# Other slots between the scans for a state-space layer's neighbouring work, and exponentials four slots ahead

## The chip, the cores and the metric

The kernel is one launch on one core of a Trainium2 chip. The metric is the device time of that launch in microseconds. TensorE (PE) multiplies and transposes, VectorE (DVE) and ScalarE (ACT) do elementwise work, GpSimd (POOL) too, and SyncE (SP) starts transfers. Each engine runs its own instructions in their order and waits on semaphores for the others.

## The reference

A decoder layer in float32: a state-space block, a cross-attention and a mixture of experts, each behind a layer norm and with a residual. The change lies in the state-space block alone:

```
xz = einsum('bld,ed->ble', layernorm(x), in_proj_w);  xp, z = xz[..., :ED], xz[..., ED:]
xc = silu(causal depthwise conv of xp over 4 positions)
dt, Bm, Cm = split(einsum('ble,fe->blf', xc, x_proj_w))
delta = softplus(dt @ dt_proj_w.T + dt_proj_b);  A = -exp(A_log)
dA = exp(delta[..., None] * A);  BX = delta[..., None] * Bm[:, :, None, :] * xc[..., None]
hs[t] = dA[t] * hs[t-1] + BX[t]
y = einsum('blen,bln->ble', hs, Cm) + D * xc
x = x + einsum('ble,de->bld', y * silu(z), out_proj_w)
```

x is 4 x 1024 x 256, ED is 512, there are N = 16 states and R = 64 ranks of dt.

## The kernel before, in words

`mamba_phase` cuts the 4 x 1024 positions into NCH = 8 chunks of 512 positions (CT), two to a sequence. Channels lie on partitions: ED = 512 gives KE = 4 blocks. A chunk has STEPS = 64 scans, one for each state n and block e; scan k is one VectorE instruction over 512 positions (`scan`, L485). Every scan is the centre of one **slot**. Each engine's program is written by the same double loop, `slots`: chunk h, slot s, and for each slot the function `slot` of that engine, which puts the slot's own instructions first and then whatever of other work has that slot's number.

For scan k the engines do this. ScalarE computes the decay, `a_step` (L369, exp of delta times A), into `a_ring`, six tiles deep, AHEAD slots ahead of the scan, and the input in turned form, `scale_u` (L381), into `bxT`, KE slots further ahead. TensorE turns bxT into one of two PSUM banks one slot ahead (`bx`, L576). VectorE scans. GpSimd multiplies two scans' results by C in one instruction, `pair` (L324), into `hc_ring`. TensorE turns and sums these products in PSUM, `y` (L593), LAG = 5 slots behind. The exponential of scan k waits until scan k-6 has left the ring; the turn for scan k until scan k-2 has left its bank.

Between these stands the work of the neighbours, by a table of slot numbers. While chunk h is scanned, chunk h+1 is prepared: XT turns the normalised input (TensorE, copied by ScalarE), IN projects it (two matmuls in two slots for each of four blocks), CONV is VectorE's convolution in four steps from the slot named, Z projects the gate (two slots for each of four tiles; VectorE copies it two slots later, L542), at SILU_AT ScalarE does a silu of xc (L433) and of zT (L437) with a table load before and after, XP projects xc to dt, B and C (four slots; ScalarE copies it to `xd_rows` four slots later, L361), BT turns those rows, DT projects dt (VectorE takes the minimum one slot later, L548, ScalarE the exponential and logarithm of the softplus, L386 and L390, VectorE the maximum four slots later, L552), U is GpSimd's delta times xc (L350), UT turns it and ScalarE copies it to `uT` (L361). Of chunk h-1, GATE multiplies y by silu(z) (L530), YT turns it, OUT projects it (four slots for each half, L684; VectorE adds the residual four slots after its number, L560). Of chunk h+2, LN takes the norm's statistics, AGGR aggregates them (L520), EPS adds the epsilon (L523, L524), RSTD is ScalarE's root (L400, L402), APPLY is GpSimd's four normalising instructions (L332). D adds D * xc (L602).

IN, Z, XP, DT, UT, YT, OUT, XT and BT share two PSUM banks (`bank_of`). The tuple `order` gives the order in which they fill them; every fill waits until the one before in its bank is emptied (`wait_emptied`).

The attention and the experts follow; the first parts of the attention stand in the last slots (`ATTEND_AT`).

## Time and profile before

| | |
|---|---|
| runs | 2038.38 us median of 3 (2036.39 to 2042.06) |
| profiled execution | 2040.1 us, its span 2038.0 us |
| PE busy | 1864.1 us, 91% of the span |
| DVE busy | 1166.3 us, 57% |
| ACT busy | 1101.7 us, 54% |
| POOL busy | 1100.7 us, 54% |
| mean granted TensorE clock | 0.978 |

Matmul busy time counts pipelined instructions by modelled ends, so a busy PE is not PE at its peak. The shares are over the whole span; the state-space part is the first 43% of it. A timeline row gives the start, the time taken, the engine and the line, what is written from what, and in brackets how long the engine had been idle and who ended that. Consecutive instructions of one kind are one row with their count. Durations of instructions that follow each other without a gap overlap by some 0.1 us, so the distance of two starts is the better measure. A "chunk" below is a value of h, its slots are counted from 0.

### The profile page before, as it was taken

The numbers are of one execution on the slowest core, as the hardware profiler recorded it, in microseconds if no ns is written. First come the engines' busy times: TensorE is split into PE (matmuls) and PEld (weight loads), VectorE is DVE, ScalarE is ACT, GpSimd is POOL, SyncE is SP. The second block draws the span as 40 slices with busy tenths as digits, with TensorE's granted clock in tenths as the row PEclk, the third lists the DMA queues.
The fourth block names the chain that finished last, engine by engine and source line by source line (L and its number), as shares of the span: only waits on it lengthen the run. The fifth ranks groups of instructions, "written<-read, shape, count | busy, mean of one in ns | idle before, by whom it ended". The sixth has DMA issues, their size and how long they took to land. (4 is left out here: it accounts for less than half of the span.)

```text
span 2038.0 us, 29493 instructions
## 1 busy us (share of the span) xinstructions
PE 1864.1 (91%) x10630; PEld 1518.1 (74%) x10630; DVE 1166.3 (57%) x1760; ACT 1101.7 (54%) x2157; POOL 1100.7 (54%) x806
## 2 busy tenths in 40 slices
PE   5888998989998998878999993999999999999998
PEld 2666676767676767766666652888888888888897
DVE  4899998999999998975677763111111111111111
ACT  3898989898989989944767761111111111111111
POOL 1686878778787878845667874222222222222131
PEclk8999999999999999999999995999999999999999
DMA  4121211112121113101111012974344444434451
GB/s 118 36 64 42 64 52 64 53 42 73 43 73 43 63 43 96 48 22 47 32 32 53 22 43 59 358 244 145 107 137 120 113 145 109 142 114 112 137 153 16
DMA packets 100019, 177.21 MB, mean 87 GB/s; under 512 B 24307, under 2 KB 70771, under 8 KB 89876
## 3 DMA queue, kind: packets, MB, share of 16 engines
q1 hardware_dynamic: 84196, 156.63, 22.9%
q0 software_dynamic: 15680, 18.69, 5.5%
q8 instruction: 87, 1.43, 0.3%
q14 instruction: 56, 0.46, 0.1%
HBM read 152.81 MB, written 22.82 MB: 86 GB/s over the span
## 5 line engine op out<-in xcount | busy, mean ns | idle before, releaser
L324 POOL TENSOR_TENSOR m_hc_ring<-m_h_ring,m_c_bc 128x1024 f32<-128x1024 f32 x256 | 606.3, 2374 | 127.8 <-DVE m_h_ring L485 109.6
L1825 PE MATMUL e_ps<-e_xT,e_w 128*128 128x256 f32 (+1 forms) x2560 | 501.0, 356 | 0.8 <-ACT e_xT L1753 0.8
L1825 PEld LDWEIGHTS e_ps<-e_xT,e_w 128*128 128x128 f32 x2560 | 440.9, 191 | 51.3 <-issue 1.2
L1737 POOL DMA_INDIRECT out<-e_y,e_who x71 | 113.4, 1597 | 552.3 <-DVE e_y L1789 449.5
L576 PEld LDWEIGHTS m_ps<-m_ident,m_bxT 128*128 128x128 f32 x2048 | 234.8, 141 | 216.6 <-DVE m_h_ring L485 102.6
L369 ACT ACTIVATE m_a_ring<-m_delta,m_negA 128x512 f32<-128x512 f32 x512 | 366.1, 716 | 39.5 <-DVE m_h_ring L485 39.1
L576 PE MATMUL m_ps<-m_ident,m_bxT 128*128 128x128 f32 x2048 | 320.6, 279 | 67.8 <-DVE m_h_ring L485 61.7
L381 ACT ACTIVATE m_bxT<-m_uT,m_bT 128x512 f32<-128x512 f32 x512 | 364.5, 712 | 0.0
L1780 DVE TENSOR_TENSOR e_hT<-e_gact,e_ps 128x512 f32<-128x512 f32 x142 | 97.7, 688 | 453.5 <-ACT e_gact L1762 453.5
L485 DVE TENSOR_TENSOR_SCAN m_h_ring<-m_a_ring,m_carry,m_ps 128x512 f32<-128x512 f32 x256 | 316.8, 1267 | 27.4 <-ACT m_a_ring L369 13.3
L485 DVE TENSOR_TENSOR_SCAN m_h_ring<-m_a_ring,m_ps 128x512 f32<-128x512 f32 x256 | 304.1, 1209 | 35.7 <-PE m_ps L576 14.1
L593 PE MATMUL m_ps<-m_ident,m_hc_ring 128*128 128x128 f32 x2048 | 309.5, 276 | 0.8
L1762 ACT ACTIVATE e_gact<-e_ps 128x512 f32<-128x512 f32 x142 | 84.8, 597 | 414.5 <-PE e_ps L1825 414.5
L1838 PE MATMUL e_ps<-e_w,e_hT 128*128 x1136 | 251.8, 379 | 1.6 <-issue 1.6
L593 PEld LDWEIGHTS m_ps<-m_ident,m_hc_ring 128*128 128x128 f32 x2048 | 242.9, 142 | 2.5 <-DVE m_zT L530 2.4
L1838 PEld LDWEIGHTS e_ps<-e_w,e_hT 128*128 128x128 f32 x1136 | 215.1, 190 | 30.6 <-issue 1.7
L1753 ACT ACTIVATE e_xT<-e_ps 128x512 f32<-128x512 f32 (+1 forms) x40 | 22.0, 549 | 260.0 <-PE e_ps L1812 260.0
L1789 DVE TENSOR_SCALAR e_y<-e_ps,e_meta 128x256 f32<-128x256 f32 x71 | 31.5, 480 | 194.4 <-PE e_ps L1838 194.4
L1031 ACT ACTIVATE t_probs<-m_ps,t_nmax 128x77 f32<-128x77 f32 x512 | 118.6, 369 | 10.1 <-DVE t_nmax L1208 10.1
L937 POOL TENSOR_TENSOR t_probs<-t_probs,t_rtotal 128x616 f32<-128x616 f32 x64 | 77.8, 1217 | 82.9 <-DVE t_rtotal L1202 80.5
L1505 PE MATMUL m_ps<-t_k_blk,t_qT 128*128 128x308 f32 x256 | 78.8, 430 | 7.0 <-ACT t_qT L1120 4.1
L1728 POOL DMA_INDIRECT e_xg<-xn,e_who x71 | 71.1, 1001 | 20.7 <-POOL e_who L1725 11.0
(195 smaller groups left out, 2077.4 us busy)
## 6 DMA issues: line engine op xcount, KB each, us to landing
e_w<-in_gate_up_w SPq DMA_DIRECT2D x78, 1024.0 KB, 6.8
m_c_bc<-c_rows SPq DMA_DIRECT2D x32, 1024.0 KB, 6.0
e_w<-in_down_w SPq DMA_DIRECT2D x8, 1024.0 KB
m_x_in<-in_x SPq DMA_DIRECT2D x8, 512.0 KB, 5.7
m_x_res<-in_x SPq DMA_DIRECT2D x8, 512.0 KB, 6.7
x<-m_x_res SPq DMA_DIRECT2D x8, 512.0 KB, 2.9
t_xa<-x SPq DMA_DIRECT2D x8, 512.0 KB
out<-t_xa SPq DMA_DIRECT2D x8, 512.0 KB
```

Of the source, the lines that this page charges most:

```text
L324: p.tensor_tensor(hc_ring[:, k % HC, :, :], h_ring[:, n % 2, e:e + 2, :], c_bc[:, n, :].unsqueeze(1).to_broadcast([P, 2, CT]), ALU.mult).t ...
L369: a.activation(a_ring[:, k % A_RING, :], delta[c % 2][:, e, :], ACT.Exp, scale=negA[:, e, n:n + 1]).then_inc(a_ready, 1)
L381: a.activation(bxT[:, row % BXT, i, :], uT[c % 2][:, i, :], ACT.Copy, scale=bT[:, c % 2, i, n:n + 1]).then_inc(bxT_ready, 1)
L485: v.tensor_tensor_scan(h_ring[:, n % 2, e, :], a_ring[:, k % A_RING, :], ps[:, BX + k % 2, :], initial, ALU.mult, ALU.add).then_inc(scan_d ...
L576: last = t.transpose(out[:, i * P:(i + 1) * P], src(i), ident[:])
L593: last = t.matmul(ps[:, Y + i, e * P:(e + 1) * P], hc_ring[:, k // 2 % HC, e % 2, i * P:(i + 1) * P], ident[:], is_transpose=True, start=( ...
L1031: last = a.activation(dst[:, h, :], src[:, h // (HP // 2), h % (HP // 2), :], ACT.Exp, bias=nmax[:, g % 2, h:h + 1])
L1737: nc.gpsimd.indirect_dma_start(out=out, out_offset=bass.IndirectOffsetOnAxis(ap=who[:, tile:tile + 1], axis=0), in_=y[:, s % 2, i, :], in_ ...
L1762: nc.scalar.activation(gact[:, k % 2, :], gu_bank(s, g, 0), ACT.Gelu).then_inc(g_ready, 1)
L1780: nc.vector.tensor_tensor(h_out(s, g), gact[:, k % 2, :].rearrange("p (f t) -> p f t", f=n), gu_bank(s, g, 1).rearrange("p (f t) -> p f t" ...
L1825: last = t.matmul(gu_bank(s, g, which)[:, f * wide:(f + 1) * wide], w1[s % W1_RING][:, c, lo:lo + P], xT[:, s % 2, c, 0:wide], start=(c == ...
L1838: last = t.matmul(ps[:, Y_BANK + s % 2, i * D:(i + 1) * D], hT[:, s % 2, f, i * P:(i + 1) * P], w2[:, bass.ds(e, 1), f, :].rearrange("p a ...
```

## The change

The number of instructions stays; the table of slots and one constant change. The exponential (and with it bxT) is placed four slots ahead of its scan instead of three. CONV of the first block moves from slot 9 to 8, the second Z tile from 27 to 26, XP from 30 to 27, BT from 35 to 32, DT, U and UT three slots earlier (the last two UT: 49 and 51 become 46 and 48), the first half of OUT from 51 to 50. AGGR and EPS move from 56 and 57 to 60, RSTD from 59 to 62, APPLY from 60 to 63. `order` is now computed from the same table by sorting, with the result in the order of the slots.

```
--- before.py
+++ after.py
@@ -110,7 +110,7 @@
     TOTAL = NCH * STEPS
     ONE_ROW, C0, B0 = R, R + 32, R + 32 + N
     A_RING, BXT, HC = 6, 3, 4
-    AHEAD, LAG = 3, 5
+    AHEAD, LAG = 4, 5
     TAIL = KC - 1
     G = 4
     NG = N // G
@@ -182,9 +182,24 @@
 
         bank_of = {"XT": (0, 1), "IN": (0, 1, 0, 1), "YT": (0, 0, 0, 0), "Z": (1, 0, 1, 0), "XP": (1,), "BT": (0,),
                    "DT": (1, 0, 1, 0), "UT": (1, 0, 1, 0), "OUT": (1, 0)}
-        order = (("XT", 0), ("XT", 1), ("IN", 0), ("IN", 1), ("IN", 2), ("IN", 3), ("YT", 0), ("YT", 1), ("YT", 2),
-                 ("YT", 3), ("Z", 0), ("Z", 1), ("XP", 0), ("BT", 0), ("DT", 0), ("DT", 1), ("DT", 2), ("DT", 3),
-                 ("UT", 0), ("UT", 1), ("UT", 2), ("UT", 3), ("OUT", 0), ("OUT", 1), ("Z", 2), ("Z", 3))
+        LN_AT, AGGR_AT, EPS_AT, RSTD_AT, APPLY_AT = (51, 52, 53, 54), 60, 60, 62, 63
+        XT_AT = (1, 2)
+        GATE_AT = (5, 6)
+        IN_AT, CONV_AT = (5, 9, 13, 17), (8, 13, 17, 21)
+        D_AT = (7, 11, 15, 19)
+        YT_AT = (21, 22, 23, 24)
+        SILU_AT = 25
+        Z_AT = (25, 26, 59, 61)
+        XP_AT, BT_AT = 27, 32
+        DT_AT = (33, 34, 38, 39)
+        U_AT = (38, 39, 43, 45)
+        UT_AT = (43, 44, 46, 48)
+        OUT_AT = (50, 55)
+
+        fill_at = {"XT": XT_AT, "IN": IN_AT, "YT": YT_AT, "Z": Z_AT, "XP": (XP_AT,), "BT": (BT_AT,), "DT": DT_AT,
+                   "UT": UT_AT, "OUT": OUT_AT}
+        order = sorted(((kind, i) for kind, at in fill_at.items() for i in range(len(at))),
+                       key=lambda f: fill_at[f[0]][f[1]])
         nth, fills = {}, [0, 0]
         for h in range(-1, NCH + 1):
             for kind, i in order:
@@ -210,20 +225,6 @@
                         attend(g)
             for g in range(0, parts.last):
                 attend(g)
-
-        LN_AT, AGGR_AT, EPS_AT, RSTD_AT, APPLY_AT = (51, 52, 53, 54), 56, 57, 59, 60
-        XT_AT = (1, 2)
-        GATE_AT = (5, 6)
-        IN_AT, CONV_AT = (5, 9, 13, 17), (9, 13, 17, 21)
-        D_AT = (7, 11, 15, 19)
-        YT_AT = (21, 22, 23, 24)
-        SILU_AT = 25
-        Z_AT = (25, 27, 59, 61)
-        XP_AT, BT_AT = 30, 35
-        DT_AT = (36, 37, 41, 42)
-        U_AT = (41, 42, 46, 48)
-        UT_AT = (46, 47, 49, 51)
-        OUT_AT = (51, 55)
 
         block = ctx.enter_context(nc.Block())
```

On TensorE, from the second half of the first Z tile to the first XP matmul. L654 is the z projection, L663 the x projection (line numbers of the changed kernel are one higher), L576 the turn of bxT, L593 that of the products; one turn and one product stand in each slot. Before:

```order
L654 MATMUL m_ps<-m_w_in,m_xnT 128x512
L576 MATMUL m_ps<-m_ident,m_bxT 128x128 x4
L593 MATMUL m_ps<-m_ident,m_hc_ring 128x128 x4
L654 MATMUL m_ps<-m_w_in,m_xnT 128x512
L576 MATMUL m_ps<-m_ident,m_bxT 128x128 x4
L593 MATMUL m_ps<-m_ident,m_hc_ring 128x128 x4
L654 MATMUL m_ps<-m_w_in,m_xnT 128x512
L576 MATMUL m_ps<-m_ident,m_bxT 128x128 x4
L593 MATMUL m_ps<-m_ident,m_hc_ring 128x128 x4
L576 MATMUL m_ps<-m_ident,m_bxT 128x128 x4
L593 MATMUL m_ps<-m_ident,m_hc_ring 128x128 x4
L663 MATMUL m_ps<-m_xc,m_w_x 128x512
```

And now, from the first half of the first Z tile:

```order
L655 MATMUL m_ps<-m_w_in,m_xnT 128x512
L577 MATMUL m_ps<-m_ident,m_bxT 128x128 x4
L594 MATMUL m_ps<-m_ident,m_hc_ring 128x128 x4
L655 MATMUL m_ps<-m_w_in,m_xnT 128x512 x2
L577 MATMUL m_ps<-m_ident,m_bxT 128x128 x4
L594 MATMUL m_ps<-m_ident,m_hc_ring 128x128 x4
L655 MATMUL m_ps<-m_w_in,m_xnT 128x512
L664 MATMUL m_ps<-m_xc,m_w_x 128x512
L577 MATMUL m_ps<-m_ident,m_bxT 128x128 x4
L594 MATMUL m_ps<-m_ident,m_hc_ring 128x128 x4
L664 MATMUL m_ps<-m_xc,m_w_x 128x512
```

Four z matmuls in four slots, a free slot and then the x projection have become z matmuls in three slots with two of them in the second, and the x projection begins in the third.

On ScalarE, at the start of the first chunk's scans, behind the copies of uT. L369 is the exponential (a_ring), L381 is bxT, L400 and L402 are the norm's root. Before:

```order
L361 ACTIVATE m_uT_82<-m_ps 128x4x128 x4
L381 ACTIVATE m_bxT<-m_uT_82,m_bT 128x512 x3
L400 ACTIVATE m_rstd<-m_rstd 128x4
L402 ACTIVATE m_rstd<-m_rstd 128x4
L381 ACTIVATE m_bxT<-m_uT_82,m_bT 128x512
L369 ACTIVATE m_a_ring<-m_delta_80,m_negA 128x512
L381 ACTIVATE m_bxT<-m_uT_82,m_bT 128x512
L369 ACTIVATE m_a_ring<-m_delta_80,m_negA 128x512
```

And now:

```order
L362 ACTIVATE m_uT_82<-m_ps 128x4x128 x4
L382 ACTIVATE m_bxT<-m_uT_82,m_bT 128x512 x4
L370 ACTIVATE m_a_ring<-m_delta_80,m_negA 128x512
L382 ACTIVATE m_bxT<-m_uT_82,m_bT 128x512
L370 ACTIVATE m_a_ring<-m_delta_80,m_negA 128x512
L382 ACTIVATE m_bxT<-m_uT_82,m_bT 128x512
L370 ACTIVATE m_a_ring<-m_delta_80,m_negA 128x512
L382 ACTIVATE m_bxT<-m_uT_82,m_bT 128x512
L401 ACTIVATE m_rstd<-m_rstd 128x4
L403 ACTIVATE m_rstd<-m_rstd 128x4
L370 ACTIVATE m_a_ring<-m_delta_80,m_negA 128x512
```

The root stood behind three bxT; it now stands behind seven bxT and three exponentials.

## Rows read from the trace of the kernel before

**Rows 1.** Busy time by stretch (us, PE, PEld, DVE, ACT, POOL, PEclk, DMA share, GB/s)
```profile
56.40:885.90 829.50, 754.84 (x5176) 597.22 (x5173) 761.96 (x819) 756.21 (x1202) 660.48 (x396) 0.99 0.18 54
163.60:206.10 42.50, 38.40 (x280) 30.63 (x279) 42.50 (x50) 33.51 (x55) 30.26 (x13) 1.00 0.18 50
206.10:249.50 43.40, 38.98 (x259) 28.80 (x257) 39.65 (x40) 43.36 (x68) 35.40 (x18) 1.00 0.22 66
249.50:270.30 20.80, 20.80 (x136) 17.47 (x137) 18.05 (x25) 19.74 (x34) 17.03 (x12) 1.00 0.13 45
```

**Rows 2.** Timeline of ScalarE, chunk 1 (start us, us, engine, line, operation, count)
```profile
205.94 1.28 ACT L433 ACT_TABLE_LOAD   x1
...
212.27 0.72 ACT L369 ACTIVATE m_a_ring<-m_delta,m_negA 128x512 f32<-128x512 f32 x1
...
222.09 0.71 ACT L369 ACTIVATE m_a_ring<-m_delta,m_negA 128x512 f32<-128x512 f32 x1
```

**Rows 3.** Timeline of VectorE, chunk 1 (in brackets: idle before, and its releaser)
```profile
213.02 1.28 DVE L485 TENSOR_TENSOR_SCAN m_h_ring<-m_a_ring,m_carry,m_ps 128x512 f32<-128x512 f32 x1 [1.55 <-ACT m_a_ring L369]
...
261.53 1.28 DVE L485 TENSOR_TENSOR_SCAN m_h_ring<-m_a_ring,m_carry,m_ps 128x512 f32<-128x512 f32 x1 [0.46 <-PE m_ps L576]
```

**Rows 4.** Timeline of TensorE, chunk 1 and the start of chunk 2
```profile
205.59 0.66 PE L576 MATMUL m_ps<-m_ident,m_bxT 128*128 128x128 f32 x4 [0.30 <-DVE m_h_ring L485]
...
206.52 1.02 PE L654 MATMUL m_ps<-m_w_in,m_xnT 128*128 128x512 f32 x2
...
224.04 0.66 PE L576 MATMUL m_ps<-m_ident,m_xd_rows 128*128 128x128 f32 x4 [0.68 <-ACT m_xd_rows L361]
...
249.47 1.10 PE L684 MATMUL m_ps<-m_w_out,m_ygT 128*128 128x256 f32 x4 [0.61 <-ACT m_uT L361]
...
259.10 0.60 PE L576 MATMUL m_ps<-m_ident,m_bxT 128*128 128x128 f32 x4
...
260.84 0.60 PE L576 MATMUL m_ps<-m_ident,m_bxT 128*128 128x128 f32 x4
...
272.52 0.60 PE L576 MATMUL m_ps<-m_ident,m_x_in 128*128 128x128 f32 x4
```

**Rows 5.** Timeline of ScalarE, chunk 1: copies of xd_rows and of uT
```profile
223.32 0.66 ACT L361 ACTIVATE m_xd_rows<-m_ps,m_xd_bias 128x512 f32<-128x512 f32 x1
...
248.75 0.57 ACT L361 ACTIVATE m_uT<-m_ps 128x512 f32<-128x512 f32 x1
```

**Rows 6.** Timeline of VectorE, chunk 1, behind the last max of the softplus
```profile
242.42 5.96 DVE L485 TENSOR_TENSOR_SCAN m_h_ring<-m_a_ring,m_carry,m_ps 128x512 f32<-128x512 f32 x5
```

**Rows 7.** Timeline of GpSimd, chunk 1
```profile
242.57 1.28 POOL L350 TENSOR_TENSOR m_u<-m_delta,m_xc 128x512 f32<-128x512 f32 x1
...
262.89 2.38 POOL L324 TENSOR_TENSOR m_hc_ring<-m_h_ring,m_c_bc 128x1024 f32<-128x1024 f32 x1 [1.10 <-DVE m_h_ring L485]
265.25 2.18 POOL L332 TENSOR_SCALAR m_x_in<-m_x_in,m_nmean,m_rstd 128x256 f32<-128x256 f32 x4
```

**Rows 8.** Timelines of ScalarE and TensorE at the start of chunk 0
```profile
52.70 1.95 ACT L381 ACTIVATE m_bxT<-m_uT,m_bT 128x512 f32<-128x512 f32 x3
...
62.85 0.57 ACT L361 ACTIVATE m_xnT<-m_ps 128x512 f32<-128x512 f32 x1
...
65.22 1.66 PE L639 MATMUL m_ps<-m_xnT,m_w_in 128*128 128x512 f32 x2 [1.98 <-ACT m_xnT L361]
```

**Rows 9.** Timeline of VectorE, chunk 7, behind the silu
```profile
842.36 3.73 DVE L485 TENSOR_TENSOR_SCAN m_h_ring<-m_a_ring,m_carry,m_ps 128x512 f32<-128x512 f32 x3 [2.13 <-ACT m_a_ring L369]
```

**Rows 10.** Timelines of VectorE and GpSimd, chunk 0, at the epsilon
```profile
149.73 0.85 DVE L523 TENSOR_SCALAR m_rstd<-m_mv 128x4 f32<-128x4 f32 x1
150.50 2.40 DVE L524 TENSOR_SCALAR m_nmean<-m_mv 128x4 f32<-128x4 f32 x1
...
158.30 1.22 DVE L485 TENSOR_TENSOR_SCAN m_h_ring<-m_a_ring,m_ps 128x512 f32<-128x512 f32 x1 [1.91 <-PE m_ps L576]
...
148.17 4.70 POOL L324 TENSOR_TENSOR m_hc_ring<-m_h_ring,m_c_bc 128x1024 f32<-128x1024 f32 x2
```

## The prediction

> **What bounds the kernel now.** The view by stage comes first. The state-space part is the stretch from 56.4 to 885.9 us, 829.5 of 2038.0 us [rows 1]; the order of its work is all that the diff touches, so what follows it can only shift as a whole. In that stretch VectorE is busy for 762.0 us and ScalarE for 756.2, GpSimd for 660.5 and TensorE for 754.8: four engines of nearly equal load. So not the sum counts but which of them is late at which slot. Chunk 1, cut in three, shows it [rows 1]: in the first 42.5 us (slots 0 to 24, convolution) VectorE has no gap at all; in the next 43.4 (slots 25 to 50) ScalarE has none; in the last 20.8 (from slot 51, output and z projections) TensorE has none. The timelines of the engines show the joints. ScalarE does the two silus with a table load ahead and one behind, from 205.94 to 212.27, before the next exponential [rows 2]; the scan of slot 29 waits for that exponential, idle 1.55 us [rows 3]. In a slot with a projection TensorE turns bxT and the products (0.93 us, from 205.59 to 206.52) and multiplies 512 columns (0.87 more): in all 1.74 us once it has no waits, as from 259.10 to 260.84 [rows 4]. A scan takes 1.18 us (five from 242.42 to 248.30 [rows 6]), so every slot with a projection and no other VectorE work costs 0.55 us of VectorE's time. The last joint is the start of the output projection: TensorE stands at 249.47 for a copy of uT on ScalarE, which came at 248.75 [rows 4, 5]. From there twelve projection slots follow each other at 1.74 us.
>
> **The change, part by part.** No instruction is added or removed. One slot is the step between two scans.
>
> AHEAD 3 to 4: ScalarE writes one exponential and one bxT more before the silus. An exponential with its bxT takes 1.225 us (eight such pairs lie between the exponentials of 212.27 and 222.09). So at 212.27 the exponential of slot 30 stands where that of slot 29 stood. The wait of 1.55 [rows 3] is thereby not won: the z and x projections now stand in slots 25 to 30 without a free slot, two in slot 26 and two in slot 27. From 205.59, TensorE needs 1.82 + 2.61 + 2.61 + 1.74 us up to the turn for slot 30, that is to 214.4, and a scan starts 0.69 after its turn begins (260.84 and 261.53 [rows 3, 4]): 215.1. With the old wait it is 213.02 and a scan and a copy later, 214.8. The wait changes its name there, from ScalarE to TensorE.
>
> x projection, turn of its rows, softplus, u and its turns three slots earlier: ScalarE meets each of these three pairs sooner. The copy of xd_rows goes from 223.32 to 223.32 - 3 x 1.225 = 219.65, the copy of uT for which the output waits from 248.75 to 245.08 [rows 5], ready at 245.65. TensorE's wait for xd_rows (0.68, [rows 4]) stays: by the steps above it arrives in slot 32 at 219.66 and the rows at about 220.3. The last max of the softplus needs ScalarE's last logarithm, so it also comes 3.7 us sooner: it ended as the scan of 242.42 began [rows 6], now at 238.7, but in slot 43, not 46. The scans of slots 44 to 49 follow: 6 x 1.18, to 245.8. TensorE turns for slot 51 and turns the product, 0.9, and the output projection begins at 246.7 in place of 249.47. The uT it needs is there 1.0 us sooner. From its start to the next chunk are twelve slots at 1.74, as before, and one slot without a projection (54, since the output now begins in slot 50): 0.87. **A full chunk gains 2.8 - 0.87 = 1.9 us**, six chunks (1 to 6) 11.6. Both ends: nothing, if something else holds slot 49; and the whole 2.8.
>
> Convolution from slot 8, not 9: its first step now waits for the D term of slot 7, one slot earlier instead of two. TensorE needs 0.44 (turn), 0.87 (two products) and 0.87 (D) for it, 2.2 us; VectorE is there after the scans of slots 7 and 8, 2.36. VectorE is without a gap in this stretch [rows 1], and does the same work in another slot: 0. SyncE's store of the C rows follows the copy of xd_rows and comes 3.7 us sooner; its loads wait for GpSimd's products of the chunk, as before: 0.
>
> Norm: aggregate and epsilon in slot 60 (56 and 57), the root in 62, the apply in slot 63 (59, 60). The apply ran at 265.25 for 2.18 us, and its first reader, TensorE's turn, at 272.52 [rows 4, 7]: 5.1 us of slack. It now stands behind one product more, which waits for the scan of slot 61: 3.5 us later (two slots at 1.74). 1.6 us of slack are left: 0. In the first chunk it is not 0. There ScalarE's order decides: the root stood behind the three bxT of 52.70 [rows 8], now it stands behind ten operations, seven more, 4.3 us later. TensorE then waits in slot 1 for about 3 us. The scans behind are held less, since IN waits for the copies of xnT anyway: the copy stood at 62.85 behind 16 such operations and stands behind 18 now: + 1.2 us, and with it the projection that waited until 65.22 [rows 8]. By the count above the scans up to slot 49 give back 0.2 (245.96 and 245.8). **Chunk 0: 1.0 us slower.** Chunk 7 has no projections of a neighbour: there the wait of 2.13 behind the silu [rows 9] loses the whole extra pair: **1.2 us faster**.
>
> Where VectorE's epsilon meets GpSimd is the open price. In chunk 0 the two tiny operations took 0.85 and 2.40 us, ending as GpSimd's two products ended that began at 148.17, and the scan behind waited 1.91 more for TensorE [rows 10]; four columns alone are worth about 0.2 each. In the other chunks they fell into GpSimd's gap. In slot 60 the first meets the product of slots 58 and 59: that starts with the end of scan 59 and runs 2.38 [rows 7], the epsilon comes 2.1 after it (one slot of 1.74 and 0.36 for the aggregates). 0.3 us of waiting, under 0.5 of VectorE's slack per projection slot: 0. The ends are 0 and 4.8 (0.85 + 2.40 - 2 x 0.2 + 1.91) a chunk; GpSimd's gap of 1.10 ahead of each product in this stretch [rows 7] is the nearest row, so 0. For chunk 0, where it was already paid, the same.
>
> The Trainium skill ("SBUF — State Buffer", section "Who interferes with whom") says that a tensor_scalar that uses both port pairs and GpSimd hold the shared pair for a whole instruction and that the other fully blocks. By that rule two products that follow each other would stop both operations of the epsilon, one would stop only the first. The trace agrees where they meet, in chunk 0 [rows 10].
>
> **Sum:** -11.6 - 1.2 + 1.0 = -11.8 us against the profiled execution's own 2040.1: 2028.3. That execution lies 1.7 above the median of the runs, 2038.4; against the median it is 2026.6. Even chunks' scans start without a carry and are a little shorter, which the count leaves out: I give **2026**.
>
> **The rivals.**
> *More comes back.* Chunk 0 loses its stall of 4.8 us, since slots 59 to 62 at 1.74 let GpSimd catch up. For it: GpSimd is behind only where slots are short. Against: there two products ran one behind the other [rows 10], so it was far behind. 2026 - 5 = 2021.
> *GpSimd holds slot 49.* u and the products alternate on it: 1.28 and 2.38 [rows 7]. By my count the product that TensorE turns in slot 49 is ready at 244.8 and wanted at 245.1. If it is one u (1.3 us) later, the output begins 1.0 later and a chunk gains 1.0: 6 x 1.0 + 0.2 = 6.2, 2032.
> *Slower: the epsilon is stopped twice in every chunk.* If in slot 60 a second product stands ready when the first ends, each of five chunks (those that prepare a norm between scans, chunk 0 having paid already) pays 4.8: +24, 2050. It decides as soon as GpSimd is more than 1.4 us behind the scans. For it: chunk 0 [rows 10] and the new place in an even slot. Against: TensorE sets the pace there, and GpSimd has a gap of about 1.1 us in every 3.47.
> That the change does not do what it says is excluded: the orders show the moves.
>
> **How the numbers follow.** 0.3% is 6.1 us, about what a measurement of this kernel can tell from no change. My forecast (gain of 7 to 19): 0.60. More comes back: 0.13. GpSimd holds slot 49 (gain of 2 to 8): 0.18, a quarter of it faster by over 6.1. Slower: 0.09. That gives 0.77 faster, 0.14 same, 0.09 slower. The range takes the first three cases: from 2017 (2.8 a chunk and chunk 0's stall gone would be 2016) to 2035.
>
> **What would show it.** In the changed profile: a steady chunk of about 104.7 us from scan to scan in place of 106.7; no wait of the scan for ScalarE behind the silu but gaps for TensorE in slots 28 to 35; no wait of the output projection for the uT copy; the epsilon's second operation at 0.16 us in chunks 1 to 5; a later root, and a longer wait of TensorE, in chunk 0; a wait of about 1 us in chunk 7. Wrong would be: chunks still at 106.7, an epsilon over 1 us, or a TensorE wait for x_in in each chunk.

## The result and the profile after

| | before | changed |
|---|---|---|
| median of the runs, us | 2038.61 (2036.39 to 2042.06, 4 runs) | 2019.92 (2019.32 to 2020.12, 4 runs) |
| profiled execution, own time / span | 2040.1 / 2038.0 | 2020.12 / 2018.1 |
| mean granted clock | 0.978 | 0.978 |
| state-space part | 56.4 to 885.9: 829.5 | 56.4 to 867.6: 811.2 |
| attention and experts | 1152.1 | 1150.5 |

Changed to before: 0.9906, 95% interval 0.9889 to 0.9923, so 18.7 us faster. Of the 19.9 us between the two spans 18.3 lie in the state-space part. Over the fourteen kernels profiled here, all with the same attention and experts, attention takes 384.9 to 389.6 us (up to the experts' first product with their weights, L1826 of the changed kernel) and the experts 763.9 to 765.3; the 1.6 us found there are inside that scatter and are not counted to the change.

Busy time by stretch in the changed kernel, columns as in [rows 1]: the whole state-space part, then slots 25 to 49 without the silus, then from the start of the output projection to the next chunk.

```profile
56.40:867.60 811.20, 750.82 (x5175) 599.35 (x5172) 760.62 (x820) 757.32 (x1203) 660.57 (x398) 0.99 0.18 55
...
208.40:242.40 34.00, 30.97 (x219) 24.08 (x217) 31.15 (x30) 34.00 (x60) 28.07 (x14) 1.00 0.22 63
242.40:271.00 28.60, 28.38 (x200) 24.28 (x198) 27.25 (x35) 27.34 (x47) 24.89 (x21) 1.00 0.23 76
```

The busy times are those of [rows 1], within 4.1 us on TensorE and 1.4 on the others. The 18 us went out of idle time, not out of work. The groups of VectorE's scans over the state-space part say so (last columns: busy us, mean ns | idle before, and what ended it), before:

```profile
L485 DVE TENSOR_TENSOR_SCAN m_h_ring<-m_a_ring,m_carry,m_ps 128x512 f32<-128x512 f32 x253 | 313.1, 1267 | 27.3 <-ACT m_a_ring L369 13.3 <-issue 6.5 <-PE m_ps L576 6.4
L485 DVE TENSOR_TENSOR_SCAN m_h_ring<-m_a_ring,m_ps 128x512 f32<-128x512 f32 x256 | 304.1, 1209 | 35.7 <-PE m_ps L576 14.1 <-issue 10.6 <-ACT m_a_ring L369 10.3
```

and after:

```profile
L486 DVE TENSOR_TENSOR_SCAN m_h_ring<-m_a_ring,m_carry,m_ps 128x512 f32<-128x512 f32 x253 | 311.9, 1266 | 20.7 <-PE m_ps L577 11.5 <-issue 4.6 <-ACT m_a_ring L370 4.0
L486 DVE TENSOR_TENSOR_SCAN m_h_ring<-m_a_ring,m_ps 128x512 f32<-128x512 f32 x256 | 302.3, 1207 | 24.5 <-PE m_ps L577 14.0 <-ACT m_a_ring L370 5.2 <-issue 4.8
```

The idle time falls by 6.6 and 11.2, 17.8 in all. In both groups together the waits for ScalarE go from 23.6 to 9.2, while those for TensorE rise from 20.5 to 25.5: the wait has partly changed its name.

A full chunk is measured from its first gate to the next one's. (The gate multiplies the finished chunk's y by silu(z), in slot 5 of the next chunk.) Timeline of VectorE, before and then after:

```profile
170.68 1.26 DVE L530 TENSOR_TENSOR m_zT<-m_ps,m_zT 128x512 f32<-128x512 f32 x2
...
277.21 1.26 DVE L530 TENSOR_TENSOR m_zT<-m_ps,m_zT 128x512 f32<-128x512 f32 x2
```

```profile
166.28 1.26 DVE L531 TENSOR_TENSOR m_zT<-m_ps,m_zT 128x512 f32<-128x512 f32 x2
...
270.99 1.26 DVE L531 TENSOR_TENSOR m_zT<-m_ps,m_zT 128x512 f32<-128x512 f32 x2
...
374.12 1.26 DVE L531 TENSOR_TENSOR m_zT<-m_ps,m_zT 128x512 f32<-128x512 f32 x2
```

Chunk 0 with the start ends 4.40 earlier (170.68 and 166.28). Odd chunks go from 106.53 to 104.71, even ones from 105.45 to 103.13, which makes 12.4 over the six. Chunk 7, to the first operation of the attention, goes from 79.3 to 77.8. Together 18.3.

The joints of chunk 1 in the changed kernel, on ScalarE:

```profile
201.54 1.28 ACT L434 ACT_TABLE_LOAD   x1
...
207.86 0.72 ACT L370 ACTIVATE m_a_ring<-m_delta,m_negA 128x512 f32<-128x512 f32 x1
...
243.57 0.58 ACT L362 ACTIVATE m_uT<-m_ps 128x512 f32<-128x512 f32 x1
```

on VectorE:

```profile
208.95 1.28 DVE L486 TENSOR_TENSOR_SCAN m_h_ring<-m_a_ring,m_carry,m_ps 128x512 f32<-128x512 f32 x1 [0.66 <-PE m_ps L577]
```

and on TensorE:

```profile
215.95 0.66 PE L577 MATMUL m_ps<-m_ident,m_xd_rows 128*128 128x128 f32 x4 [0.58 <-ACT m_xd_rows L362]
...
242.45 1.03 PE L685 MATMUL m_ps<-m_w_out,m_ygT 128*128 128x256 f32 x4
```

The scan behind the silus, which waited 1.55 for ScalarE [rows 3], now waits 0.66 for TensorE. Three more waits of 0.45 or 0.46 for TensorE follow, and one of 0.54 for which the profile names nobody. The turn of xd_rows still waits, 0.58 for 0.68 [rows 4]. The output projection no longer waits for uT. It starts 76.17 behind the chunk's first gate; before it was 78.79 (249.47 [rows 4] less 170.68), 2.62 more. The norm's late apply still comes in time: in the full chunks it ends 1.4 us ahead of TensorE's turn of it (264.9 and 266.3), where 5.1 lay between them before; 1.6 was forecast.

The start of chunk 0 in the changed kernel, ScalarE, TensorE, VectorE:

```profile
58.54 0.20 ACT L403 ACTIVATE m_rstd<-m_rstd 128x4 f32<-128x4 f32 x1
...
63.56 0.57 ACT L362 ACTIVATE m_xnT<-m_ps 128x512 f32<-128x512 f32 x1
```

```profile
61.06 1.11 PE L577 MATMUL m_ps<-m_ident,m_x_in 128*128 128x128 f32 x4 [2.73 <-POOL m_x_in L333]
...
66.85 1.02 PE L640 MATMUL m_ps<-m_xnT,m_w_in 128*128 128x512 f32 x2
```

```profile
63.14 1.22 DVE L486 TENSOR_TENSOR_SCAN m_h_ring<-m_a_ring,m_ps 128x512 f32<-128x512 f32 x1 [3.30 <-PE m_ps L577]
...
152.31 2.40 DVE L524 TENSOR_SCALAR m_rstd<-m_mv 128x4 f32<-128x4 f32 x1
...
154.62 0.16 DVE L525 TENSOR_SCALAR m_nmean<-m_mv 128x4 f32<-128x4 f32 x1
```

The root is late and TensorE waits for the normalized rows, as forecast, but the input projection then runs without a wait and in 1.02, where before it waited 1.98 and took 1.66 [rows 8]. At the chunk's end the epsilon is held once instead of twice [rows 10], and the scan behind it waits for nothing. GpSimd at that place, products of 128x1024:

```profile
147.49 4.72 POOL L325 TENSOR_TENSOR m_hc_ring<-m_h_ring,m_c_bc 128x1024 f32<-128x1024 f32 x2
...
152.29 2.39 POOL L325 TENSOR_TENSOR m_hc_ring<-m_h_ring,m_c_bc 128x1024 f32<-128x1024 f32 x1
155.97 2.37 POOL L325 TENSOR_TENSOR m_hc_ring<-m_h_ring,m_c_bc 128x1024 f32<-128x1024 f32 x1 [1.30 <-DVE m_h_ring L486]
```

### The profile page after: what moved, and what is told of

The parts are those of the page before. It is cut to its first block and busy times, and to the rows that moved or that the text cites. A ratio compares the mean times of both kernels' runs of the same rounds, so it can differ in the third digit from the quotient of the medians.

```text
span 2018.1 us, 29493 instructions
## 1 busy us (share of the span) xinstructions
PE 1861.4 (92%) x10630; PEld 1521.3 (75%) x10630; DVE 1164.5 (58%) x1760; ACT 1102.9 (55%) x2157; POOL 1098.7 (54%) x806
## 5 line engine op out<-in xcount | busy, mean ns | idle before, releaser
L1826 PE MATMUL e_ps<-e_xT,e_w 128*128 128x256 f32 (+1 forms) x2560 | 502.1, 357 | 1.0 <-ACT e_xT L1754 0.8
L1826 PEld LDWEIGHTS e_ps<-e_xT,e_w 128*128 128x128 f32 x2560 | 441.4, 191 | 52.1 <-issue 1.1
L1533 PE MATMUL m_ps<-t_pT,t_v_all 128*128 128x512 f32 (+1 forms) x160 | 81.4, 608 | 0.8 <-ACT t_pT L1041 0.8
```

The source lines that it names most:

```text
L1826: last = t.matmul(gu_bank(s, g, which)[:, f * wide:(f + 1) * wide], w1[s % W1_RING][:, c, lo:lo + P], xT[:, s % 2, c, 0:wide], start=(c == ...
```

## The experiments

Each ratio is to the kernel before, whose medians beside these runs were 2038.4 to 2039.7; differences from the changed kernel are to its median of 2019.92. Lengths of segments are differences of the scans' starts on VectorE's timeline; a start inside a merged row is interpolated, so a figure is good to 0.04. Chunk 0 is measured from its first scan (it starts between 56.3 and 60.3) to the first gate. Each length is of one profiled execution. In the tables "norm only" is the norm alone, "chain only" the chain from the x projection to the output projection alone, "bias" the kernel with the epsilon as ScalarE's bias.

| us, chunk 0 by slots | before | changed | ahead 4 only | norm only | chain only | norm back | bias |
|---|---|---|---|---|---|---|---|
| 0 to 12 | 22.71 | 22.14 | 23.76 | 21.97 | 22.72 | 25.00 | 22.21 |
| 13 to 40 | 46.33 | 48.35 | 46.36 | 46.33 | 48.34 | 48.35 | 48.36 |
| 41 to 48 | 12.70 | 10.36 | 12.69 | 12.70 | 10.35 | 10.35 | 10.45 |
| 49 to 54 | 7.98 | 7.98 | 7.99 | 7.98 | 7.98 | 7.99 | 8.05 |
| 55 to 59 | 9.04 | 5.54 | 9.21 | 5.54 | 9.09 | 9.51 | 5.54 |
| 60 to first gate | 15.51 | 15.50 | 15.11 | 15.28 | 15.66 | 16.13 | 14.25 |
| sum | 114.27 | 109.87 | 115.12 | 109.80 | 114.14 | 117.33 | 108.86 |

| us, chunk 1 by slots | before | changed | ahead 4 only | output from 51 | output from 49 |
|---|---|---|---|---|---|
| 0 to 24 | 42.48 | 42.47 | 42.47 | 42.47 | 42.48 |
| 25 to 32 | 12.58 | 13.69 | 11.62 | 13.69 | 13.68 |
| 33 to 40 | 13.23 | 14.24 | 14.20 | 14.24 | 14.25 |
| 41 to 48 | 12.88 | 10.60 | 12.88 | 10.59 | 10.60 |
| 49 to 54 | 9.80 | 9.36 | 9.79 | 8.51 | 9.88 |
| 55 to 59 | 8.81 | 7.58 | 8.81 | 8.81 | 7.29 |
| 60 to 63 | 6.93 | 6.94 | 6.93 | 6.94 | 7.22 |

How far the start scatters can be seen on three kernels that share every slot up to the first gate: the changed one and those with the output projection from slots 51 and 49. Their slots 0 to 12 took 22.14, 21.3 and 22.4, the sum to the first gate 109.9, 108.9 and 110.2. The rows from slot 13 on agree among them within 0.05. So a difference of under about 1.2 us in the first row of the first table tells nothing by itself.

### Four slots ahead, alone; and the table without it

The kernel before with

```diff
-    AHEAD, LAG = 3, 5
+    AHEAD, LAG = 4, 5
```

> Only the count AHEAD is 4 instead of 3; the whole table of slots is that of the kernel before. Theory 1 (ScalarE's list between the silus and the last copy of uT holds the same number of pairs of exponential and bxT product whatever AHEAD is, and this list sets the start of the output projection): full chunks unchanged (output projection of chunk 1 at 249.5 +- 0.3, chunks 106.5 and 105.5 in turn), chunk 7 shorter by 1.2, so 2037 (2036 to 2038). Rival (the scan's wait for ScalarE behind the silus, 1.55 in the profile before, is won in each chunk once the pairs are a slot earlier): 6 x 1.55 + 1.2 = 10.5 less, 2028, and the first gate of a chunk 1.5 earlier than the last one's place each time.

Measured: 2040.60, ratio 1.0014 (1.0004 to 1.0023). Full chunks 106.53 and 105.45, as before within 0.02: theory 1 holds for them, and the rival does not. The scan of slot 29 no longer waits:

```profile
212.76 1.28 DVE L486 TENSOR_TENSOR_SCAN m_h_ring<-m_a_ring,m_carry,m_ps 128x512 f32<-128x512 f32 x1 [0.16 <-issue]
```

What slots 25 to 32 win, 0.96, slots 33 to 40 give back, 0.97. Chunk 7 is 1.2 shorter, the start of chunk 0 1.05 longer. The total is 3.6 above theory 1 and outside its range; the start is 1.05 of that, and where the rest lies is not known: the profiled execution ends 0.2 before that of the kernel before.

The changed kernel with the same line turned round:

> The whole changed table of slots, AHEAD left at 3. Theory 1: all of the gain but that of chunk 7 stays: 2019.9 + 1.2 = 2021 (2020 to 2022.5), the first gates of chunks 1 to 6 at the changed kernel's distances (103.1 to 104.7), chunk 7 at 79.3 instead of 77.8. Rival (a fourth pair ahead carries the scan over the silus in each chunk, and the table alone has the 1.55 wait back as lost time): 6 x 1.55 + 1.2 = 10.5 lost, 2030.

Measured: 2023.09, ratio 0.9923 (0.9906 to 0.9939). First gate at 164.70, full chunks 104.71 and 103.13, chunk 7 at 78.5. The fourth pair is worth nothing in the full chunks, in either table. In chunk 0 it costs (from the first scan 109.9 with it and 108.0 without), in chunk 7 it gives. This kernel's state-space part even ends 0.9 before the changed kernel's, at 866.7; its longer time is in the attention, 389.6 against 385.3, which nothing here explains. The median is 2 above the 2021 of theory 1, and still far from the rival's 2030.

### The norm alone, and the chain alone

The kernel before with

```diff
-        LN_AT, AGGR_AT, EPS_AT, RSTD_AT, APPLY_AT = (51, 52, 53, 54), 56, 57, 59, 60
+        LN_AT, AGGR_AT, EPS_AT, RSTD_AT, APPLY_AT = (51, 52, 53, 54), 60, 60, 62, 63
```

> Only the norm's four places are the changed ones (60, 60, 62, 63); all else as before. Theory 1: the steady chunks have slack before the transposed copies and change by 0 +- 0.2 each; chunk 0 wins what the two traces show there, 4.4 less about 0.6 which came from the earlier projections: 2038.6 - 3.8 = 2035 (2033.5 to 2036.5), with no 2.40 stall of the scan's engine in chunk 0's second half. Rival A (my forecast for chunk 0: later root, later copies, 1.0 lost): 2039.6. Rival B (chunk 0's gain comes from the earlier chain, not from the norm): 2038.6 +- 0.5.

Measured: 2033.96, ratio 0.9979 (0.9970 to 0.9989). Full chunks 106.52 and 105.46. Theory 1 (2035) is right. Chunk 0 wins 4.47: 0.74 at the start, which is within the scatter, and 3.50 in slots 55 to 59. The run moves all four places of the norm together; that the 3.50 are the epsilon's is read from its rows. Chunk 7 is 1.3 shorter (78.0), of which more below.

The kernel before with

```diff
-        XP_AT, BT_AT = 30, 35
+        XP_AT, BT_AT = 27, 32
-        DT_AT = (36, 37, 41, 42)
+        DT_AT = (33, 34, 38, 39)
-        U_AT = (41, 42, 46, 48)
-        UT_AT = (46, 47, 49, 51)
-        OUT_AT = (51, 55)
+        U_AT = (38, 39, 43, 45)
+        UT_AT = (43, 44, 46, 48)
+        OUT_AT = (50, 55)
```

> Only the chain is earlier: x projection, B's turn, step size, u, uT three slots earlier, output projection from slot 50; AHEAD 3, and the z projection, convolution and norm in their old slots. Theory 1: the full chunks' 12.4 stays, chunk 7 +0, chunk 0's stall stays: 2038.6 - 12.4 = 2026 (2024.5 to 2028). Rival (the chunks' gain needs all parts together: the gate, z and AHEAD): under half of it, 2032 or more. If this and the norm alone (2035) add up to the whole table at AHEAD 3 (2021), the parts are independent: 2038.6 - 12.4 - 3.8 = 2022.4.

Measured: 2025.48, ratio 0.9935 (0.9919 to 0.9952). Full chunks 104.72 and 103.25: the earlier chain is the whole gain of the odd chunks and 2.2 of the even chunks' 2.3. Chunk 0 gains 0.1. No run moves the second Z tile and the first convolution alone; in the full chunks they are what lies between this kernel and the whole table at three slots ahead, 0.0 and 0.1. Up to the attention the norm alone wins 5.6 (it begins at 880.3), the chain alone 13.8 (872.2) and the whole table at three slots ahead 19.2 (866.7). That the first two add up to the third is in part chance: chunk 7 runs 1.3 faster in each of the single ones by its clock (last section), and the third has a start of chunk 0 that is 1.7 shorter than with the norm alone.

### The changed kernel with the norm back

The changed kernel, norm at 56, 57, 59, 60.

> The changed kernel with the norm's four places back at 56, 57, 59, 60. Theory 1 (the norm's move is worth 4.2 in chunk 0 alone, as the first gates show: 170.68 before, 166.45 with the norm alone moved): 2019.9 + 4.2 to 5.5 = 2024 to 2025.5, first gate at 170.5 to 171.8, all later chunks at the changed kernel's lengths. Rival (with the chain already early the norm's place no longer matters): 2020 to 2021.

Measured: 2025.48, ratio 0.9935 (0.9919 to 0.9952). Chunk 0 is 7.46 longer than the changed one: 2.86 at the start, 3.97 in slots 55 to 59; the first gate is at 173.60, where theory 1 had at most 171.8. So the norm's late place is worth more beside the fourth pair (7.5) than without it (4.5), and the difference is over the scatter. At the start TensorE waits, and then projects slowly:

```profile
66.48 2.05 PE L640 MATMUL m_ps<-m_xnT,m_w_in 128*128 128x512 f32 x2 [3.20 <-ACT m_xnT L362]
...
69.18 1.91 PE L640 MATMUL m_ps<-m_xnT,m_w_in 128*128 128x512 f32 x2
```

At the chunk's end the epsilon's first operation is held past two of GpSimd's products in a row, and its second not at all; VectorE, then GpSimd:

```profile
151.56 3.39 DVE L524 TENSOR_SCALAR m_rstd<-m_mv 128x4 f32<-128x4 f32 x1
154.87 0.15 DVE L525 TENSOR_SCALAR m_nmean<-m_mv 128x4 f32<-128x4 f32 x1
...
150.25 4.68 POOL L325 TENSOR_TENSOR m_hc_ring<-m_h_ring,m_c_bc 128x1024 f32<-128x1024 f32 x2
```

### Only the start's root early

In the changed kernel, in the passes ahead of chunk 0 alone:

```diff
-                    if s == AGGR_AT:
+                    if s == (AGGR_AT if h >= 0 else 54):
-                    if s == EPS_AT:
+                    if s == (EPS_AT if h >= 0 else 54):
-                if s == RSTD_AT and h + 2 < NCH:
+                if s == (RSTD_AT if h >= 0 else 55) and h + 2 < NCH:
```

> The changed kernel; only ahead of chunk 0 (the pass that prepares it) the norm of chunk 1 has its epsilon at slot 54 and its root at 55, so that ScalarE does the root before the first pairs. Theory 2 (at the start TensorE waits for GpSimd's normalized rows once, the granted clock falls to 0.5 behind that wait, and it matters which work runs then: four short turns of 1.1 in all in the changed kernel, two input projection pieces of 1.66 and 1.77 before): the wait moves back to the later slots, the slow stretch falls on the input projection, and the first gate is 0.5 to 1.5 later than in the changed kernel (166.8 to 167.8), 2020.5 to 2021.5. Rival (my forecast's reason: the later root costs 1.2 at the start): the first gate 1.2 earlier, 165.1, 2018.7.

Measured: 2021.45, ratio 0.9916 (0.9900 to 0.9933); first gate 168.26. The wait is back where it was, and the slow piece behind it:

```profile
67.09 1.10 PE L640 MATMUL m_ps<-m_xnT,m_w_in 128*128 128x512 f32 x2 [2.84 <-ACT m_xnT L362]
68.61 1.91 PE L640 MATMUL m_ps<-m_xnT,m_w_in 128*128 128x512 f32 x2
```

The first gate is 1.98 later, but 1.47 of that is a first scan at 57.88 (56.41 in the changed kernel), and 1.4 is there at the first exponential of the softplus (41.60 and 40.21), before the root's place is reached. The 0.5 that are left are inside the scatter, so this run does not show what the placement of the slow stretch is worth; the placement itself came as expected. What the run does refute is my forecast's reason, that the late root costs 1.2 at the start: an early one gains nothing.

### The output projection one slot later, and one earlier

The changed kernel with `OUT_AT = (51, 55)`:

> The changed kernel with the output projection from slot 51 instead of 50. Theory 1 (what counts is the number of slots that hold a projection and the number of light ones between; one more light slot before the projection costs a scan's pace, but the projection's twelve slots are the same ones by TensorE's time): the projection waits for nothing in both, and slot 54 then has a projection again, so it starts a slot later and nothing is lost or won: 0 +- 1, 2020. Rival A (each slot of start is worth 0.87 as in my forecast): 6 x 0.87 = 5.2 slower, 2025. Rival B (less TensorE idle at slot 54): 6 x 0.87 faster, 2015.

Measured: 2025.05, ratio 0.9935 (0.9918 to 0.9951). Rival A is nearest by the runs; by the trace full chunks are 105.07 and 103.67, 0.36 and 0.54 longer, 2.5 us up to the attention. Its start, and below that of the kernel with slot 49:

```profile
243.34 1.03 PE L685 MATMUL m_ps<-m_w_out,m_ygT 128*128 128x256 f32 x4
```

```profile
242.00 1.06 PE L685 MATMUL m_ps<-m_w_out,m_ygT 128*128 128x256 f32 x4
```

The projection starts 1.23 later behind the gate (243.34 - 165.94 = 77.40) and has one slot without a projection less (0.87): 0.36 is what is left, and 0.36 is what chunk 1 shows. So theory 1 is wrong by that much, and rival A's 0.87 a chunk too. The rest of the 5.1 us between the medians is outside the state-space part or did not fall into the profiled execution.

The changed kernel with `OUT_AT = (49, 54)`:

> The changed kernel with the output projection from slots 49 and 54 instead of 50 and 55: light slots at 53 and 58. The kernel with slots 51 and 55 (eight slots of projection in a row) had full chunks of 105.07 and 103.67 against 104.71 and 103.13, 0.45 a chunk longer by the traces. Theory 1 (what the light slot between the two halves gives is a place for work that is late, and one such place is enough): no change, full chunks within 0.2 of the changed kernel's, 2020. Rival A (each slot earlier is worth something again): 6 x 0.45 to 6 x 0.87 less, 2015 to 2017.5. Rival B (the projection now waits for ScalarE's copy of the turned u, which ends at 241.2 in chunk 1 of the changed kernel against a start of 242.45): 2022 or more, with a wait for ScalarE ahead of the projection's first piece.

Measured: 2027.65, ratio 0.9947 (0.9930 to 0.9963). Rival B has the time, but not for its reason; the other two are wrong. Full chunks are 105.21 and 103.92, longer by 0.5 and 0.8. There is no wait for the copy of uT; the first piece starts 1.03 sooner (242.00 - 166.86 = 75.14). A second slot, 58, is now without a projection: + 0.87. And the epsilon meets GpSimd's product:

```profile
259.51 1.00 DVE L524 TENSOR_SCALAR m_rstd<-m_mv 128x4 f32<-128x4 f32 x1
```

against 0.33 in the changed kernel, + 0.67. Together -1.03 + 0.87 + 0.67 = 0.51. That is chunk 1's number, but as a split it is argued: in the even chunks the same terms give 0.56 of the 0.8. Chunk 6, which prepares no norm and so has no epsilon, is longer by only 0.27 (103.38 and 103.11), so about 0.5 of an even chunk's 0.8 goes with the epsilon. Slot 50 is the best of the three.

### Epsilon off VectorE

The changed kernel with

```diff
-                        v.tensor_scalar(rstd[:], mv[:, :, 1], EPS, None, ALU.add).then_inc(ln_step, 1)
-                        v.tensor_scalar(nmean[:], mv[:, :, 0], -1.0, None, ALU.mult).then_inc(ln_step, 1)
...
-                    a.activation(rstd[:], rstd[:], ACT.Ln).then_inc(log_done, 1)
+                    a.activation(rstd[:], mv[:, :, 1], ACT.Ln, bias=eps_col[:]).then_inc(log_done, 1)
...
-                        p.tensor_scalar(x_in[:, i, :], x_in[:, i, :], nmean[:, i:i + 1], rstd[:, i:i + 1],
-                                        ALU.add, ALU.mult).then_inc(xn_ready, 1)
+                        p.tensor_scalar(x_in[:, i, :], x_in[:, i, :], mv[:, i, 0:1], rstd[:, i:i + 1],
+                                        ALU.subtract, ALU.mult).then_inc(xn_ready, 1)
```

> The changed kernel in which VectorE has no part in the norm's root: ScalarE's logarithm adds epsilon as its bias, GpSimd subtracts the mean itself, and the two operations of VectorE in slot 60 are gone. Theory 1 (VectorE is what the scans of slots 60 to 63 wait for, and chunk 0's first operation is held 2.40 by GpSimd's product): chunk 0 minus 2.4, each of chunks 1 to 5 minus its two operations 0.33 + 0.16, so 2.4 + 5 x 0.49 = 4.8 less, 2015. Rival (TensorE's projection sets the pace of these slots in the steady chunks and the operations hide beside it): minus 2.4 alone, 2017.5. If chunk 0's held time was hidden too: 2020.

Measured: 2034.01, ratio 0.9978 (0.9969 to 0.9988), 14 slower than the changed kernel. None of the three expectations holds: GpSimd's normalization took 1218 ns (median of 32) instead of 552, and TensorE waited for it eight times instead of twice. This kernel changes both the form (subtract) and the tile that is read (mv, two values per row). To tell the one from the other:

```diff
-                        v.tensor_scalar(nmean[:], mv[:, :, 0], -1.0, None, ALU.mult).then_inc(ln_step, 1)
+                        v.tensor_scalar(nmean[:], mv[:, :, 0], 1.0, None, ALU.mult).then_inc(ln_step, 1)
...
-                                        ALU.add, ALU.mult).then_inc(xn_ready, 1)
+                                        ALU.subtract, ALU.mult).then_inc(xn_ready, 1)
```

> The changed kernel, VectorE's second operation multiplies the mean by 1 instead of -1 and GpSimd's normalization subtracts it (subtract, then multiply) instead of adding it; the same bytes and the same tiles. Theory 3 (the subtracting form takes 1219 ns instead of 552 on GpSimd): four of them 2.67 longer, chunk 0 longer by 2.7 at the start and some at its end, the full chunks by 1.1 to 1.4, 2028 to 2034. Rival (the scalar read out of a tile with two values per row made it slow): 552 ns and 2020.

Measured: 2035.73, ratio 0.9981 (0.9971 to 0.9991), 15.8 slower than the changed kernel. That line on GpSimd (minimum/median/maximum ns) and who waited for it (us, times), this kernel and then the changed one:

```profile
L333 POOL TENSOR_SCALAR m_x_in<-m_x_in,m_nmean,m_rstd x32: 1212/1227/1234, 7.5 to 696.3; 128x256 f32<-128x256 f32 x32
...
  PE m_ps L577: 25.2, 8
```

```profile
L333 POOL TENSOR_SCALAR m_x_in<-m_x_in,m_nmean,m_rstd x32: 544/552/571, 7.6 to 680.1; 128x256 f32<-128x256 f32 x32
...
  PE m_ps L577: 12.6, 2
```

Same tiles, same bytes: the subtracting form costs 2.2 times the adding one. It is 1.4 us a chunk (106.13 and 104.51) wherever a norm is prepared: four of them are 2.7 longer, and the slack was 1.4. Chunk 6, which prepares none, keeps 103.13.

With the adding form kept, GpSimd multiplying the mean by -1 itself:

```diff
-                        v.tensor_scalar(rstd[:], mv[:, :, 1], EPS, None, ALU.add).then_inc(ln_step, 1)
-                        v.tensor_scalar(nmean[:], mv[:, :, 0], -1.0, None, ALU.mult).then_inc(ln_step, 1)
...
-                    a.activation(rstd[:], rstd[:], ACT.Ln).then_inc(log_done, 1)
+                    a.activation(rstd[:], mv[:, :, 1], ACT.Ln, bias=nmean[:, TI:TI + 1]).then_inc(log_done, 1)
...
+                    p.tensor_scalar(nmean[:, 0:TI], mv[:, :, 0], -1.0, None, ALU.mult).then_inc(negated, 1)
```

> As the last-but-one study kernel but with GpSimd's normalization in its old form (add, then multiply, 552 ns each in the changed kernel where the subtracting form took 1219): ScalarE's logarithm adds epsilon as its bias, GpSimd multiplies the mean by -1 itself (one small operation of about 0.2), VectorE's two operations of slot 60 are gone. Theory 1 (VectorE's two operations stand on the path, the first held 2.4 in chunk 0): chunk 0 minus 2.4, chunks 1 to 5 minus up to 0.5 each less GpSimd's 0.2: 2019.9 - 2.4 - 1.5 to 2.5 = 2015 to 2016. Rival (hidden in the steady chunks): 2017.5. Rival B (the subtracting form was not what cost 14 in the earlier kernel, but the root's place on ScalarE): 2030 or more.

Measured: 2020.98, ratio 0.9911 (0.9894 to 0.9927), as the changed kernel: neither of the gains that were expected, nor rival B's loss. Full chunks 104.83 and 103.14: in the steady chunks VectorE's two operations hide. Chunk 0 is 1.0 shorter, not 2.4; the held operation of 2.40 cost 1.25 in the slots from 60 (15.50 and 14.25). That TensorE worked on meanwhile is my reading of the rest.

And with three slots ahead until chunk 7:

```diff
-                if 0 <= at + AHEAD < TOTAL:
-                    a_step(at + AHEAD)
-                if 0 <= at + AHEAD + KE < TOTAL:
-                    scale_u(at + AHEAD + KE)
+                late = (NCH - 1) * STEPS
+                for k in range(at + 3 + (at > late), at + 4 + (at >= late)):
+                    if 0 <= k < TOTAL:
+                        a_step(k)
+                    if 0 <= k + KE < TOTAL:
+                        scale_u(k + KE)
```

> The kernel with epsilon as a bias, and the exponentials three slots ahead in chunks 0 to 6, four from the first slot of chunk 7. By the first gates, three slots ahead with the changed table ended chunk 0 1.6 earlier than four (164.7 against 166.3), while chunk 7 wants four (78.5 against 77.8). Theory 1 (the two are independent): another 1.6 less than the kernel with the bias alone, 2014. Rival (the gain of chunk 0 was that run's clock, or the pass after it pays it back): as the kernel with the bias alone, within 0.5.

Measured: 2017.56, ratio 0.9889 (0.9872 to 0.9905). It has the lowest median of all, but its interval and the changed kernel's overlap, so that it beats it is not settled. From the first scan chunk 0 takes 107.0, 1.8 less than with the bias alone, as three slots ahead had shown; the first scan itself came 1.5 later, at 57.99, and ate most of it. 1.4 of that is there at the first exponential of the softplus (41.65 against 40.22), where the two kernels do the same.

## Why the prediction was right, and where it was not

The forecast was 2026 (2017 to 2035), the result 2019.92: inside the range, faster by 18.7 where 12.4 were forecast.

That 18.7 falls into the forecast's own branch, a gain of 7 to 19, is in part luck: its terms for the full chunks and chunk 7 came out, and the rest of the gain belongs to a rival.

**Full chunks: right.** Forecast 1.9 each, 11.6 in all; measured 1.82 and 2.32 in turn, 12.4. The working holds on TensorE: the output projection was to start 2.8 sooner and starts 2.62 sooner, the slot without a projection was to cost 0.87, and from the projection to the next gate it is 27.74 before and 28.54 after, 0.80 more. The chain alone brings all but 0.1 of it, and output from 51 confirms the 0.87 apart from it (27.67 against 28.54). The even chunks' extra 0.5 was not in the count. By the scans of chunk 2 it lies in three places: 0.1 in slots 5 to 12, where the first convolution moved, 0.2 in slots 25 to 48 and 0.2 in slots 49 to 59; why they are these stays open. By the scans' view the gain looks different, since TensorE turns ahead of them: they are at slot 49 only 0.16 sooner (12.58 + 13.23 + 12.88 against 13.69 + 14.24 + 10.60) and win the rest behind it, 0.44 in slots 49 to 54 and 1.23 in slots 55 to 59.

**The wait behind the silus: right.** It was to change its name and did: with the fourth pair alone 0.96 is won and 0.97 given back, with the table it is a row of waits for TensorE.

**Chunk 7: right by the term.** The wait of 2.13 [rows 9] became 0.97:

```profile
825.88 2.50 DVE L486 TENSOR_TENSOR_SCAN m_h_ring<-m_a_ring,m_carry,m_ps 128x512 f32<-128x512 f32 x2 [0.97 <-ACT m_a_ring L370]
```

1.16 against a forecast of 1.2; the chunk as a whole won 1.5. Slots 55 to 58 gave 1.0 (6.96 and 5.97), and other places took some of it back.

**Chunk 0: wrong in sign.** Forecast 1.0 slower, measured 4.40 faster. This is most of the miss: between the sum of 11.8 and the 18.3 of the state-space part lie 6.5 us, and chunk 0 has 5.4 of them (the full chunks 0.8, chunk 7 0.3). Three parts:
- The copy of xnT behind 18 operations instead of 16, + 1.2: the count ahead by itself cost 1.05 with the old table and 1.9 with the new one (22.14 and 20.27 in slots 0 to 12), so its sign is right. But the later root was put at nothing. It wins 0.74 with three slots ahead, which is inside the scatter, and 2.86 with four, which is not; with all moves the start comes out 0.57 ahead. TensorE waits about 3 us in both kernels (now 2.73 and 0.54; before 0.65, 0.75 and 1.98). What I left out is what runs behind the wait, of which the last section has the rows.
- Slots 13 to 48: forecast -0.2, measured -0.32. Right.
- The epsilon, "for chunk 0, where it was already paid, the same": wrong. In slots 56 and 57 it cost 3.50 (9.04 and 5.54, the same number with the norm moved alone). In slot 60 it is still held 2.40, and costs 1.25. In slot 57 the scan behind also waited 1.91 for TensorE; in slot 60, where TensorE has projections to do, it waits for nothing. The rival "more comes back", which I gave 0.13, named this and was the truth for 3.5 of its 4.8 us. Its reason, that GpSimd would have caught up, is only half right: three products in a row ran from 147.49 to 154.68, and the hold of 2.40 is still there.

What the forecast made of the rule that it cited (the Trainium skill, "SBUF — State Buffer", section "Who interferes with whom"), that one product stops only the first of two such operations and two stop both, is borne out for one product and only in part for two. In the changed kernel one product begins at 152.29, the epsilon's first operation at 152.31; that one takes 2.40, and the next takes 0.16. Output from 49 has 1.00 and 0.16. Behind two products in a row the kernels before, ahead 4 and chain alone had both operations stopped (0.85 and 2.40, 0.84 and 2.40, 1.05 and 2.39), but with the norm back the first was held 3.39, past both products, and the second took 0.15. So the time until the last product ends can be counted; which operation pays it can't. The rival "slower", two stops in every chunk, did not come; the first operation takes 0.33 us in the odd chunks and 0.46 in the even ones, where it takes 0.15 unhindered, so it waits 0.2 to 0.3, as the forecast's 0.3 says. "GpSimd holds slot 49" did not come either: the projection starts without a wait.

## What to carry to other kernels

In a pipeline whose engines are evenly loaded, as here, count a moved step on the engine that sets the pace behind it: when its long run of work can start, and how many slots of that run are light. Moves that only fill a wait ahead of another engine's wait are given back within a few slots. A small operation's price is not its own time but what stands beside it: put it where the engine that sets the pace has work in hand (the epsilon cost 3.5 us in one slot and 1.25 in another), and check the prologue and the last pass apart from the steady ones, since there the same move can have the other sign (the fourth pair: nothing in the full chunks, a loss in chunk 0, a gain in chunk 7).

## What the runs showed of the hardware

GpSimd's 128x256 tensor_scalar with two per-row scalars took 552 ns as add and multiply, and 1218 or 1227 ns as subtract and multiply (medians of 32 each).

A 128x4 tensor_scalar of VectorE, 0.15 us by itself, took 2.40 when a product of GpSimd had begun 0.02 before it, and 3.39 when it met two products in a row.

TensorE's granted clock fell behind its wait at the start, and it matters which work runs then. At the start, before and then after (columns as in [rows 1]):

```profile
64.00:68.00 4.00, 2.78 (x7) 1.72 (x8) 1.37 (x2) 4.00 (x8) 2.08 (x1) 0.70 0.01 2
68.00:72.00 4.00, 4.00 (x28) 3.09 (x27) 2.29 (x2) 4.00 (x8) 2.52 (x2) 0.87 0.00 0
```

```profile
61.00:64.00 3.00, 2.94 (x14) 2.94 (x15) 0.86 (x1) 3.00 (x6) 2.76 (x7) 0.50 0.00 0
64.00:68.00 4.00, 3.46 (x17) 2.46 (x16) 3.50 (x4) 4.00 (x8) 3.69 (x4) 0.67 0.41 135
68.00:72.00 4.00, 4.00 (x33) 3.47 (x32) 3.30 (x4) 4.00 (x8) 3.94 (x3) 1.00 0.00 0
```

In the changed kernel the low level, 0.50 or 1.2 GHz, falls on turns (1.11 for four of them instead of 0.60), before it fell on the input projection (1.66 and 1.77 for two, instead of 1.02). The other kernels divide in the same way: in all nine with the root behind the first exponentials the first two pairs of projections take 1.02 each, in the five with an early root (before, ahead 4, chain alone, norm back, root early) one or both of them take 1.1 to 2.05.

In chunk 7 it is not so regular. Behind its first gates TensorE waits 0.5 and 1.8 us for the scans, in every kernel. Then it runs at the low level in some (before, the changed one and eight others) and at full clock in others (norm alone, chain alone, epsilon as a bias, subtracting form). The stretch behind, before and then in the kernel with the norm alone:

```profile
809.70:813.20 3.50, 3.50 (x19) 3.27 (x18) 2.90 (x3) 2.47 (x5) 1.69 (x1) 0.51 0.99 206
```

```profile
805.40:808.90 3.50, 3.37 (x31) 3.13 (x30) 3.50 (x5) 2.47 (x5) 1.64 (x1) 1.00 0.98 212
```

It is worth 1.3 us (79.3 and 78.0 for the chunk, with the wait behind the silus 2.13 and 2.14 in both). Nothing in the slot table that these kernels share sets it, and what does stays open; it is also why chunk 7's length can't be compared to better than 1.3 us between two kernels.
